# A planner's transfer rate behind attention: 170 GB/s in place of 280 in the timetable of a transformer layer with routed experts

## What is computed

```python
# attention, 16 heads of width 16, one after another
for i in range(H):
    att = einsum('btd,bsd->bts', rotary(q[:, i]), rotary(k[:, i])) * scale
    if cascade_bias is not None:
        att = att + cascade_w[i - 1] * cascade_bias
    att = softmax(where(causal, -inf, att), axis=-1)
    out_i = einsum('bts,bsd->btd', att, v[:, i])
    cascade_bias = mean(att, axis=1, keepdims=True)
x = layernorm(x + concatenate(heads) @ Wproj)
# experts: 8, each token goes to the best one
sel, rw = argmax(x @ gate_w.T), sigmoid(max(x @ gate_w.T))
for e in range(8):
    xs = x * (rw * (sel == e))[:, None]
    out = out + (xs @ w_up[e].T) * silu(xs @ w_gate[e].T) @ w_down[e].T
x = layernorm(x + out)
```

## Time and profile before

| | us |
|---|---|
| median of 3 runs | 3336.99 |
| lowest and highest | 3334.38, 3339.17 |
| span of the profiled execution | 3451.7 |
| first gather of the last group's tiles (POOL) | 3303.90 |
| last result row issued (POOL) | 3448.21 |

### The profile page before, as it was taken

How to read it: one execution, slowest core, us unless ns; L and a number is a source line. 1 busy time by engine, 2 the same in 40 slices (tenths; PEclk the granted TensorE clock), 3 DMA queues, 4 the chain that set the end, 5 groups by cost and what they waited for, 6 DMA issues and landing times. The chain is left out here.

```text
span 3451.7 us, 93100 instructions
## 1 busy us (share of the span) xinstructions
PE 3126.0 (91%) x29688; PEld 1529.3 (44%) x29688; DVE 2614.4 (76%) x7854; ACT 3085.3 (89%) x8904; POOL 2147.9 (62%) x6194
## 2 busy tenths in 40 slices
PE   6899999989999989998999999998999998898955
PEld 3333333333444434454445444444444543444644
DVE  7666666666877787887888887787888877777754
ACT  4999999999999999998999999998999999888724
POOL 5666666665666367776666677775667655565345
PEclk9999999999999999999999999999999999999986
DMA  5322322232333324343444423344434333344353
GB/s 162 97 86 72 88 71 71 74 88 79 90 101 107 103 78 127 117 122 109 131 115 124 120 84 94 114 116 131 117 93 123 113 101 84 105 121 145 110 187 125
DMA packets 270525, 370.74 MB, mean 107 GB/s; under 512 B 61654, under 2 KB 177118, under 8 KB 270033
## 3 DMA queue, kind: packets, MB, share of 16 engines
q1 hardware_dynamic: 254784, 326.39, 32.4%
q0 software_dynamic: 14976, 37.34, 3.7%
q10 hardware_dynamic: 272, 1.05, 0.1%
HBM read 259.76 MB, written 104.40 MB: 106 GB/s over the span
## 5 line engine op out<-in xcount | busy, mean ns | idle before, releaser
L1490 DVE CUSTOM_DVE_ANT_0 att_a<-scores,window 128x128 f32<-128x128 f32 (+7 forms) x2048 | 1489.6, 754 | 464.9 <-PE scores L1182 307.7
L1356 ACT ACTIVATE att_a<-att_a,neg_max 128x128 f32<-128x128 f32 (+7 forms) x2048 | 1593.0, 778 | 73.3 <-DVE neg_max L1490 69.5
L1366 ACT ACTIVATE att_t<-scores 128x1024 f32<-128x1024 f32 (+7 forms) x2048 | 1329.5, 649 | 88.6 <-PE scores L1200 61.1
L1198 PE MATMUL scores<-q_stack,k_stack 104*128 104x512 bf16 (+3 forms) x3072 | 822.5, 333 | 130.1 <-DVE neg_max L1490 74.7
L1216 PE MATMUL pv<-att_t,v_sb 128*32 128x256 f32 (+7 forms) x16384 | 917.9, 300 | 5.7 <-ACT att_t L1366 3.3
L1182 PE MATMUL scores<-k_stack,q_stack 99*128 99x512 bf16 (+3 forms) x3072 | 687.7, 331 | 67.1 <-ACT att_t L1366 39.1
L1216 PEld LDWEIGHTS pv<-att_t,v_sb 128*32 128x32 f32 x16384 | 328.9, 108 | 592.9 <-issue 549.0
L1198 PEld LDWEIGHTS scores<-q_stack,k_stack 104*128 104x128 bf16 x3072 | 258.4, 98 | 531.2 <-DVE neg_max L1490 233.9
L1200 PE MATMUL scores<-identb,mask 128*128 128x128 bf16 x2048 | 454.7, 222 | 0.0
L1816 POOL TENSOR_SCALAR biasv<-col_sum,w_cas 128x8 f32<-128x8 f32 x240 | 88.8, 370 | 552.9 <-ACT att_t L1366 540.2
L1366 ACT ACTIVATION_READ_ACCUMULATOR att_t<-scores 128x1 f32 x2048 | 424.0, 207 | 0.0
(11 more groups left out here) (345 smaller groups left out, 4342.8 us busy)
## 6 DMA issues: line engine op xcount, KB each, us to landing
runner_r<-in_experts SPq DMA_DIRECT2D x137, 384.0 KB
qk_parts<-of_proj SPq DMA_DIRECT2D x128, 384.0 KB
of_proj<-in_xt SPq DMA_DIRECT2D x29, 1024.0 KB
q_stack<-qk_parts SPq DMA_DIRECT2D x256, 96.0 KB
k_stack<-qk_parts SPq DMA_DIRECT2D x256, 96.0 KB
q_stack<-qk_parts SPq DMA_DIRECT2D x256, 64.0 KB
k_stack<-qk_parts SPq DMA_DIRECT2D x256, 64.0 KB
head_out<-o_sb SPq DMA_DIRECT2D x252, 64.0 KB
```

Of the source, the lines that this page charges most:

```text
L1198: engine.matmul(scores[:, c0:c1], ks[0:ROWS_B, j * P:(j + 1) * P], qs[0:ROWS_B, j * P + c0 - base:j * P + c1 - base], start=True, stop=True)
L1356: engine.activation(taken, taken, EXP, scale=-1.0, bias=neg_max[:, n, i:i + 1], accum_out=row_sum[:, n, i:i + 1]).then_inc(s_exp_a, 1)
L1366: engine.activation(att_t[:, ring:ring + end - base], scores[:, base:end], EXP, accum_out=col_sum[:, n, j:j + 1]).then_inc(s_exp_b, 1)
L1490: engine.tensor_tensor_reduce(out=att_a[:, ring:ring + end - base], in0=scores[:, base:end], in1=window[:, T - (end - base):T], op0=ALU.ad ...
```

## The change

One constant is added, and the two places where a size is turned into a time ask a function for the rate: 170e3 bytes per microsecond once `over[0]` is set, 280e3 before.

```diff
-    BANDWIDTH = 280e3
+    BANDWIDTH, LATE_BANDWIDTH = 280e3, 170e3
...
         def side_time(s):
             if s.kind in MOVES and MOVES[s.kind][0] == "SP":
-                return max(side_busy(s), MOVES[s.kind][2] / BANDWIDTH)
+                return max(side_busy(s), MOVES[s.kind][2] / rate())
             return side_busy(s)
+
+        def rate():
+            return LATE_BANDWIDTH if over[0] else BANDWIDTH

         def moved(kind, t, busy):
             size = MOVES[kind][2]
-            dma_free[0] = max(dma_free[0], t + busy - 0.465 + LEAD) + size / BANDWIDTH
+            dma_free[0] = max(dma_free[0], t + busy - 0.465 + LEAD) + size / rate()
             return dma_free[0] + LANDING
```

## The result

The changed kernel takes 3362.33 us in the median (3361.12 to 3365.56, 4 runs), the kernel before 3338.08 us (3334.38 to 3339.99, 4 runs): a ratio of 1.0074, 95% interval 1.006 to 1.0089. That is 24 us slower, where 10 us less were forecast. Run once more beside the kernel before on another chip, the ratio was 1.0064 (1.0042 to 1.0086).

A forecast was written before the change was run, and what follows sets the result against it. The prediction saw the final stage bound by order and by POOL, which issues all gathers and result rows (111 of 145.3 us). Terms -13.3 - 2.5 + 6 = -10 us gave 3327 us (3317 to 3333), range 3313 to 3347.

The forecast's parts named there:

- (a): Last five tiles: fairer order among runners lets tiles leave nearly in order, without gaps; -13.3 us, bounds 0 and 13.3.
- (b): End, last norms: tiles 28 to 31 normed early leave three result rows instead of seven; -2.5 us, at most 5.1.
- (c): Tiles on PE: one tile at a time, PE standing still while ACT and DVE gate; +6 us, between 0 and 15.
- Ahead of the tiles: Before 3303 us: no change of order expected except late loads of quads 30 and 31; cost 0, at most 4.8 us.
- the cover: Tiles on PE: other tiles' turns partly fill holes, POOL's 2.8 us a tile is a floor; hence 6 us, not 15.
- The clock: Tile stage: if gate and down matmuls alternate strictly, PE's granted clock falls below 0.75.
- The serial order decides: Rival, PE between gate and down matmul: product waits above about 16 us, full 15 us cost; +8 us, 3345 us; chance 0.23.
- 170 is not true for the wire: Transfers: trace shows 319 GB/s during first weight loads; 170 holds only as the mean of a stage not full.
- More than that: Rival, tiles: earlier roots and result rows shrink POOL's waits by half of 34 us; -17 us, 3320 us; chance 0.11.
- Nothing measurable: Rival, tiles: POOL's order changes but its 111 us and waits stay; 3337 us, within 5; chance 0.21.

The follow-up runs named there:

- the even order at 280: Kernel before at 280 GB/s, planner taking the lower tile number between stages of the last tiles that could start equally early: ratio 0.9988.
- The repairs of these places: Changed kernel with 12 down matmuls moved behind the next tile's gate and up: 1.0057; with 3 Newton steps and 9 norm stages moved later: 1.0058; both: 1.0056.
- 350: Changed kernel with the planner's rate behind attention at 350 GB/s in place of 170: ratio 1.0005 to the kernel before.
- the gain of 0.17%: Kernel before with the tiles' transfers planned at 400 GB/s in place of 280, each landing 4 us later: 3333.70 us, ratio 0.9983.
- one run: Changed kernel with 170 GB/s for the weight loads alone, 280 for gathers and result rows: ratio 1.0032 to the kernel before.

## Why the prediction was wrong

The prediction's sum was made of three terms, and the trace measures each:

| | forecast | measured (quick chips) |
|---|---|---|
| (a) the last five tiles | -13.3 | -5.7 |
| (b) the end | -2.5 | -2.4 |
| (c) the tiles before them | +6, at most +15 | +33.0 |
| sum | -10 | +25 |

**Ahead of the tiles**: right in the cost, 0. The order was not quite unchanged (a few neighbours on PE and DVE), and the change has two divisions in the planner, not four.

**(b)**: right in mechanism, and in size by luck: half was taken because "the batch before may still be close", and half came out for another reason. Three rows stand behind the last root instead of seven. Of the 5.1 us that four rows are worth half is lost: POOL's first row comes 4.6 us behind the last root (3348.64 to 3353.24), where in the kernel before rows of the batch ahead could start 1.9 us behind it.

**(a)**: the direction was right, the size was not. The last five products lie 20.0 us apart, not within 18. Tile 31's load still comes late on SP, behind those of tiles 32 to 35. Tiles 37 and 38, the last two, run one at a time at the lower clock, 3.95 us each. And between the products of tiles 31 and 36 (3329.51 and 3337.56) there is a hole of 8.05 us: tile 36's tanh, at 3336.95, stands in ACT's list behind two batches of norms for which ACT first waits 4.38 us, until 3333.01, and PE waits 6.47 us with the down matmul:

```profile
3305.51 0.34 SPq L2087 DMA_DIRECT2D runner_r<-in_experts  x1
3309.98 0.34 SPq L2087 DMA_DIRECT2D att_a<-in_experts  x1
...
3329.51 0.28 DVE L1775 SCALAR_TENSOR_TENSOR att_a<-att_a,scores 128x128 f32<-128x128 f32 x1
3337.24 0.29 DVE L1768 SCALAR_TENSOR_TENSOR v_sb<-v_sb,scores 128x128 f32<-128x128 f32 x1 [3.08 <-ACT v_sb L1445]
3337.56 0.29 DVE L1775 SCALAR_TENSOR_TENSOR v_sb<-v_sb,scores 128x128 f32<-128x128 f32 x1
3341.51 0.29 DVE L1775 SCALAR_TENSOR_TENSOR v_sb<-v_sb,scores 128x128 f32<-128x128 f32 x1
3345.45 0.29 DVE L1775 SCALAR_TENSOR_TENSOR v_sb<-v_sb,scores 128x128 f32<-128x128 f32 x1
```

Deeper is what the even order at 280 showed: the step "last five tiles like the 34 before" took a gap at the end for time that is free. Half of it (9.0 of 17.4 us) is paid in the tiles before.

**(c) is the step that failed.** It stood at +6 us, at most +15; it measured +33.0. The mechanism was named rightly as far as it goes, and the chain of a tile alone was even timed rightly: 4.0 us at half clock by the earlier trace rows, 3.9 to 4.1 in the changed kernel. Three things were wrong with its price.

First, the pace it was compared with. The prediction took 100.2 us for 34 tiles, 2.95 each, from the profile of the kernel before, and subtracted its terms "from the median unscaled". That profile is of a slow chip. On a quick one, where the median was measured, the first 34 tiles take 79.0 us from the first gather on, 2.32 each. By the prediction's own mean chain of 3.5 us, a serial tile then costs 1.2 us more, not 0.5; over its 31 tiles that is 37 us in place of 15, and the upper bound would have held what was measured. (The changed kernel's first 34 tiles take 3.3 us each, under the 3.5.) The chain had been read from single tiles without a hole, the pace from a stretch full of them: on slow chips the first 34 tiles take 24 to 26 us longer in either kernel (79.0 and 104.8 us, 112.0 and 136.1), some 0.7 us a tile, which made the present pace look nearly as slow as the chain. On a slow chip the chain has its holes too: there the changed kernel's first 34 tiles take 4.0 us each, and the change costs them 31.3 us, though the pace of 2.95 was right for such a chip.

Secondly, the cover. "Turns of other tiles fill part of the holes, and POOL's 2.8 us a tile is a floor for both orders" was the reason for taking 6 of 15. Both halves fell. The turn is in the hole (3265.62, 3269.56 above), and the period at that clock is 4 us with it. And POOL is a floor only for an order that keeps up with it. In the kernel before it does: POOL is busy 86.5 us of 118.4, and 78 times 0.3 us between its issues make 23 of the other 32. In the changed kernel it has the same work and 25 us more, and waits 21.5 us for the norms' moments, where it waited 5.1. An engine that bounds the kernel before need not bound it under another order.

Thirdly, what the sum held at nothing: the norms and the scaling. Under the new lists PE waits 11.2 us more for scaled inputs in the first 34 tiles, and a batch of norms ahead of a tile's gating makes its longest waits for the product. The repairs of these places gave back next to nothing, so their share stays open.

**The clock**: wrong as it was put, below 0.75 for the stage. It is 0.79 in both kernels, with PE busy for 7.4 us more on the same 468 matmuls (in the first 34 tiles it did fall, from 0.88 to 0.83):

```profile
3212.73:3331.13 118.40, 79.70 (x468) 65.16 (x468) 60.91 (x255) 58.36 (x156) 86.53 (x88) 0.79 0.59 187
```

```profile
3213.45:3356.81 143.36, 87.10 (x468) 70.85 (x468) 65.19 (x255) 59.27 (x156) 86.59 (x88) 0.79 0.50 153
```

Within the stage the alternation runs at either level, in two stretches of the changed kernel:

```profile
3262.00:3279.00 17.00, 13.43 (x48) 11.10 (x48) 6.54 (x22) 6.32 (x17) 10.62 (x11) 0.50 0.62 200
3317.00:3330.00 13.00, 9.66 (x59) 7.57 (x60) 8.57 (x27) 3.56 (x11) 4.04 (x5) 1.00 0.36 111
```

At the lower level a tile takes 3.94 us or more, at the upper 2.60 (products at 3320.28, 3322.88, 3325.49, 3328.09 on DVE). Even 2.60 is more than the 2.32 of the kernel before, so the alternation costs at either level, and much more at 1.2 GHz.

**The rivals.** "The serial order decides" had 0.23 and 3345 us. Its mark came true: waits for the product beyond 16 us (29). Its price, 15 us, was the bound that failed, and it gave half of (a) against it; so it fell short by 17 us. "170 is not true for the wire" was right and not weighed: on a quick chip the transfer engines move 236 GB/s over the whole of the first 34 tiles. The page "DMA: Bandwidth & Descriptors" of the Trainium skill (Anatomy of one DMA) describes a transfer as a fixed part of about 2 us and a short part by size. The first gather's 2.9 us on a quick chip is of that size. As a guide for the planner the runs bear it out only on one side: narrow (170) lost 0.74%, but wider than 280 changed nothing (350: 1.0005), and the gain of 0.17% came with 4 us of latency that the first gather doesn't have. "More than that" fell, since POOL's waits for sums, on which it rested, belong to the slow chip: 20 us there, in the kernel before on a quick one 0.3. "Nothing measurable" was right that the profile exaggerates what there is to win, and missed by 24 us because it saw no loss.

**The range** of 3313 to 3347 missed 3362 because its upper end was the lower half of an underpriced rival. A bound made of "all 31 tiles stand alone" was taken for safe, though its unit price was a small difference of two numbers, of which one came from a profile 115 us from the median. The prediction saw that gap, and used it only as a reason for less to win.

**Left open**: what part of the price of a serial tile, 1.4 to 1.8 us, is the wait and what part the lower clock (chain and pace differ by 0.3 us at the upper level and by 1.7 at the lower); and how the changed kernel's loss divides between the serial order on PE and the places of norms and scalings in the lists of ACT and DVE, since each alone could be repaired without winning the time back. Nor was it tried to plan at 170 with a list that is forced two tiles deep.

## What to carry to other kernels

A planner's rate is not a physical constant that gets better by being truer of the mean: what matters is the order that it yields. A full queue in the plan spaces the work out one by one, and an engine that follows its list then runs it one by one even where the data came early; before adopting such a change, count in the lists how often a chain's two halves stand side by side on the engine in the middle. Take the count as a warning and not as a price: 23 such tiles cost 11 us in one run and 22 cost 25 in another. And before costing a change by "so much a tile against the present pace", see that the profile's span is that of the timed runs. If it isn't, take the pace as unknown by that factor, in both directions.

## What the hardware showed that was not expected

The same program takes 3338 us on some chips and 3447 on others, in every run (3434 to 3458 on two slow chips, 3334 to 3346 on the quick ones). The difference is not in the clock alone. In attention PE is busy 98% of the time on a quick chip and 90% on a slow one, at a granted clock of 1.00 and 0.89. A stretch of 100 us of each, quick first:

```profile
2950.00:3050.00 100.00, 98.45 (x1000) 52.36 (x994) 88.89 (x304) 99.23 (x299) 68.70 (x217) 1.00 0.45 132
2900.00:3000.00 100.00, 89.98 (x831) 46.47 (x831) 73.00 (x236) 84.58 (x247) 57.24 (x181) 0.89 0.41 118
```

In the tiles it shows as holes of some 3 us. The same pair of instructions in the kernel before, on a quick chip and on a slow one: PE transposes, ACT copies, PE multiplies. On the quick chip the matmul follows 0.85 us behind, on the slow one 3.54 us behind, and ACT stood idle for 3.59 us of it, put down to "remote". The gap "remote" of the earlier trace rows is of this kind.

```profile
3224.51 0.38 PE L1322 MATMUL side<-ident,runner_r 128*128 128x128 f32 x2
3225.36 1.16 PE L1331 MATMUL side<-runner_r 128*128 128x128 f32 x8 [0.46 <-ACT runner_r L1429]
```

```profile
3310.62 0.38 PE L1322 MATMUL side<-ident,runner_r 128*128 128x128 f32 x2
3314.16 1.97 PE L1331 MATMUL side<-runner_r 128*128 128x128 f32 x8 [3.16 <-ACT runner_r L1429]
```

What makes these holes stays open, and so does whether they belong to the chip or to the time of the measurement.
